# Linear attention with an FP4 feed-forward block on Trainium2: all of gate ahead of all of up in each half, and a tanh that waits for gate alone

## The chip, the cores and the metric

The kernel runs on one core of a Trainium2 chip. The metric is the device time of one execution in microseconds (us); lower is better. Engines are named as the profile names them: PE is the matmul engine and PEld its weight load, DVE the vector engine, ACT the scalar engine, POOL GpSimd and SP the engine that issues the DMAs. DVEq is DVE's instruction queue: the entries that DVE's sequencer carries out itself (register arithmetic, waits, branches) before or between the instructions that it hands to the datapath. All times, counts and rows in this part are those of the kernel before.

## The reference

`x` has 8 sequences of 2048 tokens of 256 features. With `xn = layernorm(x)` the output is `x + attention(xn) + ffn(xn)`. The change lies in the feed-forward part:

```python
def fp4_linear(x, w):                        # quantize both to FP4 in blocks of 16, then multiply
    xq = fp4_quant_dequant(x)
    wq = fp4_quant_dequant(w)
    return jnp.einsum('bsk,nk->bsn', xq, wq)
gate = fp4_linear(x, w_gate)                 # 256 -> 704
y = fp4_linear(x, w_up)                      # 256 -> 704
h = jax.nn.silu(gate) * y
return fp4_linear(h, w_down)                 # 704 -> 256
```

The attention part is a causal linear attention with 16 heads of 16, in buckets of 64 tokens: softmax over q's features, exp of k, running sums of k and of k times v over the earlier buckets.

## The kernel before

The 16384 tokens are cut into 128 tiles of 128. Everything is written out by hand: each engine has one program of its own, in it a function `step(n, d)`, and semaphores with computed thresholds join the programs. A step serves several tiles at once, each at another stage: while tile k is multiplied by the gate and up weights, tile k-1 is quantized for the down projection, k+1 is projected to q, k and v, and k+2 to k+4 are normalised and quantized. Steps come in pairs (d = 0 and 1, for the two parities of the buffers). The first and last pairs are written out, and the 60 pairs between are the body of a loop: `with dve.Fori(2, NP - 2) as n` at L1004 for DVE. In a loop body the threshold of a wait depends on the loop's counter, so a register has to be worked out for it; outside of loops it is a constant.

The feed-forward of one tile goes in two halves of 352 columns. For each half:

- PE (`gate_up`, L1120) multiplies the tile, in two chunks of 128 features, by gate and up. `three_passes` (L1020) makes three matmuls per chunk and per weight, since value and weight are each split in a high and a low part. Gate's sum stands in one PSUM bank (`unit0a` or `unit1a`), up's in another (`unit0b` or `unit1b`). That is twelve matmuls for a half; the last one raises `gu_done` by one.
- ACT (`tanh_gate`, L552) waits for `gu_done` and for `ga_done` of the tile before, reads gate's bank and writes `th`.
- DVE (`gate_h`, L728) waits for tanh and makes `ga` = (th + 1) * gate; DVE (`times_up`, L738) waits for `ga_done` and makes `h` = `ga` * up.

In DVE's step the two halves stand far apart: `gate_h(k, 0)`, then three instructions of other tiles, `times_up(k, 0)`; and at the end of the step `gate_h(k, 1)`, `attention(k, par, 3)` (L723, writes `att`), `times_up(k, 1)` (L744, writes `h`). With d = 1 `times_up(k, 1)` is the last instruction of the loop's body, and what follows it is the loop's turn: register arithmetic and a branch at L1004, and the first entries of the next pass, which lead to `scale_x` (L871 to L876, writes `xq_s`).

In PE's step the second half is cut in two: chunk 0 (six matmuls), `less_xn` (L1049, one matmul that waits for ACT's `split_xnt`), chunk 1 (six matmuls). In ACT's step `tanh_gate(k, 0)` comes behind `exp_q(k + 1)` (L534, `qexp`), which waits for DVE's `shift_q` (L697, `qsh`), and `tanh_gate(k, 1)` behind both `split_xnt(k + 2)` (L513, `xnt`).

Of the semaphores that an instruction waits for it carries one itself; the others are given to entries of their own ahead of it in the queue: to the register operation that works out a threshold, where one stands there, or to an EVENT_SEMAPHORE.

Of the kernel before, what the change touches and what calls it, by code (L numbers as in the profile page):

```python
# [5 lines left out]
def linear_attention_fp4_ffn_block(nc, x, wqkv_t, wout_t, wgate, wup, wdown, out):  # L6
# [18 lines left out]
    P = 128  # L25
# [7 lines left out]
    KC = D // P  # L33
# [7 lines left out]
    FH = F // 2  # L41
# [25 lines left out]
    with ctx:  # L67
        def sb(name, shape, dt=fp32):
            return ctx.enter_context(nc.sbuf_tensor(name, shape, dt))

        def pb(name):
            return ctx.enter_context(nc.psum_tensor(name, [P, 512], fp32))

        def sem(name):
            return ctx.enter_context(nc.semaphore(name))
# [9 lines left out]
        w_gate = sb("w_gate", [P, 2, KC, F], fp16)  # L85
        w_up = sb("w_up", [P, 2, KC, F], fp16)
# [60 lines left out]
        xqt = sb("xqt", [P, 2, 2, D], fp16)  # L147
# [17 lines left out]
        unit = [[pb("unit0a"), pb("unit0b")], [pb("unit1a"), pb("unit1b")]]  # L165
# [51 lines left out]
        gu_done = sem("gu_done")  # L217
# [16 lines left out]
        def after(t, per=1, nth=None):  # L234
            nth = per if nth is None else nth
            if isinstance(t, int):
                return 0 if t < 0 else NT * per if t >= NT else t * per + nth
            return t * per + nth


        def turned(t, par):
            return t * 8 + (16 - 8 * par)

        def begun(t):
            return not isinstance(t, int) or t >= 0


        def is_tile(t):
            return not isinstance(t, int) or 0 <= t < NT
# [14 lines left out]
        def _(sp):  # L264
# [35 lines left out]
            def turn_xq(t, par):  # L300
                if not is_tile(t):
                    return
                sp.wait_ge(xq_step, after(t, 8))
                sp.sem_inc(sp_turn, 1)
                if begun(t - 2):
                    sp.wait_ge(gu_done, after(t - 2, 2))
                sp.sem_inc(sp_turn, 1)
                sp.dma_start_transpose(xqt[:, par, :, :].rearrange("p s (c k) -> p (s c) k", k=P),
                                       xq_s[:, par, :, :].rearrange("p s k -> p (s k)")).then_inc(xqt_done[par], 16)
# [11 lines left out]
            def turn(i):  # L321
                for d in range(2):
                    turn_xq(2 * i + d + 1, 1 - d)
                    turn_h(2 * i + d - 1, 1 - d)
# [8 lines left out]
            last = NT // SEQ_TILES - 1  # L333
# [108 lines left out]
        def _(act):  # L442
# [109 lines left out]
            def tanh_gate(t, half, par):  # L552
                if not is_tile(t):
                    return
                act.wait_ge(gu_done, after(t, 2, half + 1))
                if begun(t - 1):
                    act.wait_ge(ga_done, after(t - 1, 2, half + 1))
                nc.scalar.activation(th[:, half, :], unit[(par + half) % 2][0][:, 0:FH], ACT.Tanh, scale=c_g[:, :])\  # L558
                    .then_inc(tanh_done, 1)
# [16 lines left out]
            def step(n, d):  # L576
                k, par, odd = 2 * n + d, d, 1 - d
                split_att(k - 1, odd, 0)
                exp_k(k + 1, odd)
                split_att(k - 1, odd, 1)  # L580
                exp_q(k + 1, odd)
                tanh_gate(k, 0, par)
                split_xnt(k + 2, par, 0)
                normalise_waits(k + 3)
                mean_waits(n, d + 4)
                split_xnt(k + 2, par, 1)
                tanh_gate(k, 1, par)
                normalise(n, d + 3)
                mean_of(n, d + 4)
                squares_wait(k + 4)  # L590
                copy_qt(k + 1, odd)
                squares_of(n, d + 4)
                snapshot(k + 1)
# [36 lines left out]
        def _(dve):  # L630
# [107 lines left out]
            def times_up(t, half, par):  # L738
                if not is_tile(t):
                    return  # L740
                dve.wait_ge(ga_done, after(t, 2, half + 1))
                if begun(t - 2):
                    dve.wait_ge(hq_step, after(t - 2, 14, 8))
                nc.vector.tensor_tensor(h[:, par, half * FH:(half + 1) * FH], ga[:, half, :],  # L744
                                        unit[(par + half) % 2][1][:, 0:FH], ALU.mult).then_inc(h_done, 1)
# [162 lines left out]
            def step(n, d):  # L908
                k, par, odd = 2 * n + d, d, 1 - d
                scale_x(k + 1, odd)  # L910
                block_max_x(k + 2, par)
                block_max_h(k - 1, odd)
                block_scales(k - 1, odd, k + 2, par)
                max_q(k + 1, odd)
                over_scales_h(k - 1, odd)
                shift_q(k + 1, odd)
                add_up(n, d - 3, 0)
                round_h(k - 1, 0)
                over_scales_x(k + 2, par)
                round_h(k - 1, 1)  # L920
                add_up(n, d - 3, 1)
                round_h(k - 1, 2)
                gate_h(k, 0, par)
                row_factor(k - 1, odd)
                round_x(k + 2, 0)
                times_up(k, 0, par)
                round_x(k + 2, 1)
                attention(k, par, 0)
                scale_h(k - 1, odd, 0)
                scale_h(k - 1, odd, 1)  # L930
                round_x(k + 2, 2)
                attention(k, par, 1)
                attention(k, par, 2)
                gate_h(k, 1, par)
                attention(k, par, 3)
                times_up(k, 1, par)
# [56 lines left out]
            cols = lambda c, i: q_cols[:, c, i * F:(i + 1) * F].rearrange("p (o b i) -> p o b i", i=2, b=FB)  # L993
# [19 lines left out]
        def _(pe):  # L1013
# [6 lines left out]
            def three_passes(outs, stat_hi, stat_lo, hi, lo, first, last):  # L1020

                for o, m in zip(outs, hi):
                    nc.tensor.matmul(o, stat_hi, m, start=first, stop=False)  # L1023
                for o, m in zip(outs, lo):
                    nc.tensor.matmul(o, stat_hi, m, start=False, stop=False)  # L1025
                for o, m in zip(outs, hi):
                    end = nc.tensor.matmul(o, stat_lo, m, start=False, stop=last)  # L1027
                return end
# [88 lines left out]
                nc.tensor.matmul(tr32, minus16[:, :], att_t[:, par, 0, :], start=False, stop=True, skip_group_check=True)\  # L1117
                    .then_inc(att_less, 1)

            def gate_up(t, half, par, chunks=range(KC)):  # L1120
                if not is_tile(t):
                    return
                gate, up = unit[(par + half) % 2]
                pe.wait_ge(xqt_done[par], turned(t, par))
                if half == 0:
                    if begun(t - 1) and 0 in chunks:
                        pe.wait_ge(h_done, after(t - 1, 2))
                elif 0 in chunks:
                    pe.wait_ge(q_shift, after(t + 1))
                    pe.wait_ge(kv_done, after(t + 1, 3))  # L1130
                cols = slice(half * FH, (half + 1) * FH)
                for c in chunks:
                    hi, lo = ((w_gate[:, s, c, cols], w_up[:, s, c, cols]) for s in range(2))
                    last = three_passes((gate[:, 0:FH], up[:, 0:FH]), xqt[:, par, 0, c * P:(c + 1) * P],
                                        xqt[:, par, 1, c * P:(c + 1) * P], hi, lo, c == 0, c == KC - 1)
                if KC - 1 in chunks:
                    last.then_inc(gu_done, 1)

            def project_att(t, par):
# [20 lines left out]
            def step(n, d, ends=False):  # L1160
                k, par, odd = 2 * n + d, d, 1 - d
                project_qkv(k + 1, odd)
                transpose_att(k - 1, odd)
                bucket(k, par, ends)
                less_att(k - 1, odd)
                gate_up(k, 0, par)
                transpose_xn(k + 2, par)
                gate_up(k, 1, par, (0,))
                less_xn(k + 2, par)
                gate_up(k, 1, par, (1,))  # L1170
                transpose_q(k + 1, odd)
                project_att(k - 2, par)
                project_h(k - 2, par)
# [6 lines left out]
            for n in range(2):  # L1180
# [3 lines left out]
                for part in range(2):  # L1184
                    pe.wait_ge((mat_hi, mat_lo)[part][n], 1)
                    for c in range(KC):
# [4 lines left out]
                        for r in range(WR):  # L1191
                            last = nc.tensor.transpose(bank[:, r * WP:(r + 1) * WP],
                                                       q_rows[0:WP, n, part, r * D + c * P:r * D + (c + 1) * P],
                                                       ident16[0:WP, 0:WP])
# [3 lines left out]
            for i, starts in enumerate(([m * P for m in range(0, 4)], [m * P for m in range(4, 8)],  # L1198
# [7 lines left out]
                for m, at in enumerate(starts):  # L1206
                    for c in range(KC):
                        last = nc.tensor.transpose(bank[0:width, m * D + c * P:m * D + (c + 1) * P],
                                                   q_cols[:, c, at:at + width], ident16[:, :])
# [53 lines left out]
```

## Time and profile before

| | us |
|---|---|
| median of 3 runs | 1497.29 (1495.11 to 1497.63) |
| the profiled execution, its own time | 1495.11 |
| span of the profiled execution, first to last instruction | 1493.3 |
| busy in it: DVE / PE / ACT | 1434.4 / 1382.8 / 1011.0 |
| PE's granted clock, mean over the span | 0.988 |

The profile comes from one execution, the fastest of the three runs. Its own time is 1.8 us more than its span. Busy times of instructions that overlap in the pipeline are merged, so the busy time of an engine is the part of the span in which it had at least one instruction under way.

### The profile page before, as it was taken

The page shows a single profiled execution, that of the slowest core. Times are in us where ns is not written, and L with a number is a line of the kernel's source. Part 1 is how long each engine was busy: PE and PEld are TensorE (multiplying, and loading weights), DVE is VectorE, ACT ScalarE, POOL GpSimd, SP SyncE. Part 2 cuts the span into 40 slices and gives each one's busy share as a digit, 9 for nine tenths or more (in the row PEclk, how much of TensorE's full clock was granted, in tenths as well). Part 3 has the DMA queues.
Part 4 walks back from the last instruction along what each step waited for, and adds up shares of the span by engine and source line. Part 5 has one row for each costly group of instructions (what it writes and reads, how often), then busy time and mean ns, then how long its engine had stood idle before and what let it go on. Part 6 is the DMA issues. An engine that isn't in the chain of part 4 may idle for free.

```text
span 1493.3 us, 43457 instructions
## 1 busy us (share of the span) xinstructions
PE 1382.8 (93%) x10702; PEld 948.7 (64%) x10702; DVE 1434.4 (96%) x4914; ACT 1011.0 (68%) x3096; POOL 175.8 (12%) x540
## 2 busy tenths in 40 slices
PE   0259999999999999999999999999999999999997
PEld 0136666666666666666666666666666666666664
DVE  5859999999999999999999999999999999999997
ACT  1687767676767677676767676767767676767662
POOL 1520101010101101010101010110101010101000
PEclk9969999999999999999999999999999999999998
DMA  5002233333332333333333323333333333233324
GB/s 114 4 7 55 63 65 77 69 63 74 70 76 58 81 68 70 64 81 68 63 71 74 72 58 78 68 70 64 81 68 69 65 77 71 61 73 70 71 47 78
DMA packets 293241, 100.01 MB, mean 67 GB/s; under 512 B 258272, under 2 KB 292704, under 8 KB 293216
## 3 DMA queue, kind: packets, MB, share of 16 engines
q1 hardware_dynamic: 293216, 99.73, 31.8%
q8 instruction: 9, 0.15, 0.0%
q14 instruction: 16, 0.13, 0.0%
HBM read 19.99 MB, written 16.78 MB: 25 GB/s over the span
## 4 chain that ended last, share of the span: by engine, by line
DVE 53%; issue 34%; DVEq 7%; ACT 3%; PE 1%; SPq 1%; DMA 0%; POOL 0%; ACTq 0%; POOLq 0%
DVE q_rows L863 5%; DVE osum L900 4%; DVE hw L825 4%; DVE xblk L758 3%; DVE h L744 3%; DVE xw L843 2%; DVE hu L829 2%; DVE hq L835 2%; DVE hv L807 2%; DVE xq_s L876 2%; DVE att L723 1%; DVE xblk L777 1%; DVE qsh L697 1%; DVE hs_lo L883 1%; DVE xblk L769 1%
## 5 line engine op out<-in xcount | busy, mean ns | idle before, releaser
L1154 PE MATMUL outp<-w_down_cat,q_rows 128*128 128x256 f16 x1408 | 246.2, 274 | 0.0
L573 ACT ACTIVATE snap<-ctxp,mask 64x68 f32<-64x68 f32 x1024 | 236.2, 308 | 3.2
L550 ACT ACTIVATE att_t<-trp 128x256 f16<-128x256 f32 x256 | 98.3, 384 | 134.0 <-PE trp L1109 129.6
L534 ACT ACTIVATE qexp<-qsh,c_q 128x256 f32<-128x256 f32 x128 | 65.1, 508 | 147.4 <-DVE qsh L697 147.3
L398 POOL TENSOR_TENSOR var_scaled<-squares,var_mul 128x1 f32<-128x1 f32 x128 | 24.8, 194 | 1188.4 <-ACT scratch L488 1181.7
L1154 PEld LDWEIGHTS outp<-w_down_cat,q_rows 128*128 128x128 f16 x1408 | 138.3, 98 | 16.5
L1156 PE MATMUL outp<-w_down_lo,q_rows 128*128 128x256 f16 x640 | 147.6, 274 | 0.0
L513 ACT ACTIVATE xnt<-trp 128x256 f16<-128x256 f32 x256 | 96.8, 378 | 57.3 <-PE trp L1049 57.3
L751 DVE TENSOR_REDUCE hblk<-h 128x44 f32<-128x704 f32 x128 | 123.6, 966 | 0.1
L807 DVE TENSOR_TENSOR hv<-h,hblk 128x704 f32<-128x704 f32 x128 | 112.7, 881 | 0.0
L558 ACT ACTIVATE th<-unit1a,c_g 128x352 f32<-128x352 f32 x128 | 69.7, 545 | 36.3 <-PE unit1b L1027 36.3
L1087 PE MATMUL nump<-snap,qt 128*64 128x144 f32 x1024 | 91.0, 299 | 3.2 <-ACT snap L573 3.2
L558 ACT ACTIVATE th<-unit0a,c_g 128x352 f32<-128x352 f32 x128 | 69.8, 545 | 29.7 <-PE unit0b L1027 29.7
L1041 PE MATMUL trp<-ident,xn 128*128 128x128 f32 x256 | 49.4, 275 | 37.7 <-ACT xn L504 37.7
L1023 PE MATMUL unit0a<-w_gate,xqt 128*128 128x352 f16 x256 | 80.5, 315 | 3.4 <-DVE qsh L697 1.2
L1023 PE MATMUL unit1a<-w_gate,xqt 128*128 128x352 f16 x256 | 80.5, 314 | 2.9
L504 ACT ACTIVATE xn<-xring,shift,rstd 128x256 f32 (+1 forms) x128 | 75.3, 589 | 11.1 <-POOL shift L408 11.1
L1023 PE MATMUL unit1b<-w_up,xqt 128*128 128x352 f16 x256 | 80.0, 313 | 0.0
L1025 PE MATMUL unit1b<-w_up,xqt 128*128 128x352 f16 x256 | 80.0, 313 | 0.0
L1023 PE MATMUL unit0b<-w_up,xqt 128*128 128x352 f16 x256 | 80.0, 313 | 0.0
L1027 PE MATMUL unit1b<-w_up,xqt 128*128 128x352 f16 x256 | 80.0, 313 | 0.0
L1027 PE MATMUL unit0a<-w_gate,xqt 128*128 128x352 f16 x256 | 80.0, 313 | 0.0
(214 smaller groups left out, 4409.2 us busy)
## 6 DMA issues: line engine op xcount, KB each, us to landing
xring<-x SPq DMA_DIRECT2D x128, 128.0 KB, 2.7
out<-xring SPq DMA_DIRECT2D x128, 128.0 KB, 2.5
xqt<-xq_s SPq DMA_TRANSPOSE x128, 2.4
q_rows<-q_rows SPq DMA_TRANSPOSE x128, 3.5
raw_qkv<-wqkv_t SPq DMA_DIRECT2D x1, 768.0 KB, 7.7
raw_gate<-wgate SPq DMA_DIRECT2D x8, 88.0 KB
raw_up<-wup SPq DMA_DIRECT2D x8, 88.0 KB
raw_down<-wdown SPq DMA_DIRECT2D x1, 704.0 KB, 6.2
```

Source lines behind the costliest of these rows:

```text
L513: nc.scalar.activation(xnt[:, par, part, :], tr32, ACT.Copy).then_inc(xnt_split, 1)
L550: nc.scalar.activation(att_t[:, par, part, :], tr32, ACT.Copy).then_inc(att_split, 1)
L558: nc.scalar.activation(th[:, half, :], unit[(par + half) % 2][0][:, 0:FH], ACT.Tanh, scale=c_g[:, :])\
L573: nc.scalar.activation(kept[:, :, cols], sums[:, :, cols], ACT.Copy, scale=mask[rows, f, h:h + 1])\
L751: nc.vector.tensor_reduce(hblk[:, 0, :], h[:, par, :].rearrange("p (o b i) -> p b o i", b=FB, i=2), AX.XY, ALU.max, apply_absolute_value=T ...
L807: nc.vector.tensor_tensor(rows(hv[:, :]), rows(h[:, par, :]), pairs_of(hblk[:, 2, :]), ALU.mult)\
L1023: nc.tensor.matmul(o, stat_hi, m, start=first, stop=False)
L1025: nc.tensor.matmul(o, stat_hi, m, start=False, stop=False)
L1027: end = nc.tensor.matmul(o, stat_lo, m, start=False, stop=last)
L1087: last = nc.tensor.matmul(nump[rows, g * 2 * SW:(g + 1) * 2 * SW], qt[:, par, g * P + s * BUCKET:g * P + (s + 1) * BUCKET], snap[:, g, s, ...
L1154: nc.tensor.matmul(downp, hqt[:, par, m, :], w_down_cat[:, m, :], start=(m == 0), stop=False)
L1156: nc.tensor.matmul(downp, hqt[:, par, m, :], w_down_lo[:, m, :], start=False, stop=False)
```

## The change

In each half all six gate matmuls now come first and all six up matmuls after them, each group with an increment of `gu_done` at its end: four for each tile instead of two. The parameter `chunks` of `gate_up` becomes `ups`, so the second half is now cut between gate and up instead of between the chunks. Tanh waits for gate's increment. Since tanh no longer stands for up being done, `times_up` gets a wait of its own for up's increment. SP's wait ahead of a transpose into `xqt` names the same moment by its new number.

```diff
 (turn_xq, SP)
-                    sp.wait_ge(gu_done, after(t - 2, 2))
+                    sp.wait_ge(gu_done, after(t - 2, 4))
...
 (tanh_gate, ACT)
-                act.wait_ge(gu_done, after(t, 2, half + 1))
+                act.wait_ge(gu_done, after(t, 4, 2 * half + 1))
...
 (times_up, DVE)
                 dve.wait_ge(ga_done, after(t, 2, half + 1))
+                dve.wait_ge(gu_done, after(t, 4, 2 * half + 2))
                 if begun(t - 2):
                     dve.wait_ge(hq_step, after(t - 2, 14, 8))
...
 (PE)
-            def gate_up(t, half, par, chunks=range(KC)):
+            def gate_up(t, half, par, ups=(0, 1)):
...
-                gate, up = unit[(par + half) % 2]
+                pair = unit[(par + half) % 2]
...
-                for c in chunks:
-                    hi, lo = ((w_gate[:, s, c, cols], w_up[:, s, c, cols]) for s in range(2))
-                    last = three_passes((gate[:, 0:FH], up[:, 0:FH]), xqt[:, par, 0, c * P:(c + 1) * P],
-                                        xqt[:, par, 1, c * P:(c + 1) * P], hi, lo, c == 0, c == KC - 1)
-                if KC - 1 in chunks:
+                for up in ups:
+                    for c in range(KC):
+                        hi, lo = ((w_gate, w_up)[up][:, s, c, cols] for s in range(2))
+                        last = three_passes((pair[up][:, 0:FH],), xqt[:, par, 0, c * P:(c + 1) * P],
+                                            xqt[:, par, 1, c * P:(c + 1) * P], (hi,), (lo,), c == 0, c == KC - 1)
                     last.then_inc(gu_done, 1)
```

The first place is PE's loop, the second half of a tile with d = 1 (`unit0a` gate, `unit0b` up; L1049 is `less_xn`). Before:

```order
L1130 ISA [waits q_shift,xqt_done1]
L1023 MATMUL unit0a<-w_gate,xqt 128x352 [waits kv_done]
L1023 MATMUL unit0b<-w_up,xqt 128x352
L1025 MATMUL unit0a<-w_gate,xqt 128x352
L1025 MATMUL unit0b<-w_up,xqt 128x352
L1027 MATMUL unit0a<-w_gate,xqt 128x352
L1027 MATMUL unit0b<-w_up,xqt 128x352
L1048 ISA
L1049 MATMUL trp<-xnt,minus 128x256 [waits xnt_split]
L1023 MATMUL unit0a<-w_gate,xqt 128x352 [waits xqt_done1]
```

And of the change, whose lines are one higher from here on:

```order
L1131 ISA [waits q_shift,xqt_done1]
L1024 MATMUL unit0a<-w_gate,xqt 128x352 [waits kv_done]
L1026 MATMUL unit0a<-w_gate,xqt 128x352
L1028 MATMUL unit0a<-w_gate,xqt 128x352
L1024 MATMUL unit0a<-w_gate,xqt 128x352
L1026 MATMUL unit0a<-w_gate,xqt 128x352
L1028 MATMUL unit0a<-w_gate,xqt 128x352
L1049 ISA
L1050 MATMUL trp<-xnt,minus 128x256 [waits xnt_split]
L1024 MATMUL unit0b<-w_up,xqt 128x352 [waits xqt_done1]
```

All of gate stands ahead of `less_xn` and all of up behind it; number, size and waits of the matmuls are the same.

The second place is DVE's loop, the end of its body with the loop's turn (`ga` and `h` are those of the second half). Before:

```order
L731 REGISTER_ALU
L734 SCALAR_TENSOR_TENSOR ga<-th,unit0a 128x352 [waits h_done,tanh_done]
L720 REGISTER_ALU
L723 TENSOR_TENSOR att<-nump,drec 128x256 [waits att_tr,att_step]
L744 TENSOR_TENSOR h<-ga,unit0b 128x352 [waits hq_step,ga_done]
L1004 REGISTER_ALU
L1004 COMPARE_AND_BRANCH
```

And of the change:

```order
L731 REGISTER_ALU
L734 SCALAR_TENSOR_TENSOR ga<-th,unit0a 128x352 [waits h_done,tanh_done]
L720 REGISTER_ALU
L723 TENSOR_TENSOR att<-nump,drec 128x256 [waits att_tr,att_step]
L742 REGISTER_ALU [waits ga_done]
L745 TENSOR_TENSOR h<-ga,unit0b 128x352 [waits hq_step,gu_done]
L1005 REGISTER_ALU
L1005 COMPARE_AND_BRANCH
```

Of the two semaphores that `h` had, the wait for `ga_done` has gone to a new register operation ahead of it, which works out the threshold for `gu_done`; `h` now has `hq_step` and `gu_done`. The second half of a tile with d = 0 changes in the same way.

The third place is DVE's loop, `times_up` of the first half with d = 0. Before:

```order
L842 REGISTER_ALU
L843 TENSOR_SCALAR xw<-xv 128x256 [waits xq_step]
L743 REGISTER_ALU [waits ga_done]
L744 TENSOR_TENSOR h<-ga,unit0b 128x352 [waits hq_step]
L846 ISA
```

And of the change:

```order
L843 REGISTER_ALU
L844 TENSOR_SCALAR xw<-xv 128x256 [waits xq_step]
L742 ISA [waits ga_done]
L744 REGISTER_ALU [waits gu_done]
L745 TENSOR_TENSOR h<-ga,unit0b 128x352 [waits hq_step]
L847 ISA
```

Here one entry is added between the wait for `ga_done` and `h`.

## Rows read from the trace of the kernel before

**Rows 1.** The page, parts 1 and 4: busy time; the chain that ended last.
```profile
PE 1382.8 (93%) x10702; PEld 948.7 (64%) x10702; DVE 1434.4 (96%) x4914; ACT 1011.0 (68%) x3096; POOL 175.8 (12%) x540
...
DVE 53%; issue 34%; DVEq 7%; ACT 3%; PE 1%; SPq 1%; DMA 0%; POOL 0%; ACTq 0%; POOLq 0%
```

**Rows 2.** Waits of DVE, whole span: who for whom, total us, times, longest.
```profile
DVE qmax L688 <- PE unit1b L1027: 15.2, 1, 15.2
...
DVE ga L734 <- ACT th L558: 2.8, 3, 2.4
```

**Rows 3.** Waits of ACT between 200 and 1400 us.
```profile
ACT th L558 <- PE unit1b L1027: 29.7, 56, 0.5
ACT th L558 <- PE unit0b L1027: 24.1, 56, 0.4
```

**Rows 4.** Timeline of ACT, one step: start, us, instruction, idle before and releaser.
```profile
706.34 0.51 ACT L534 ACTIVATE qexp<-qsh,c_q 128x256 f32<-128x256 f32 x1 [1.21 <-DVE qsh L697]
706.75 0.54 ACT L558 ACTIVATE th<-unit0a,c_g 128x352 f32<-128x352 f32 x1
...
708.91 0.55 ACT L558 ACTIVATE th<-unit1a,c_g 128x352 f32<-128x352 f32 x1 [0.53 <-PE unit1b L1027]
```

**Rows 5.** Timeline of PE in the same step.
```profile
704.22 0.31 PE L1023 MATMUL unit0a<-w_gate,xqt 128*128 128x352 f16 x1
704.37 0.31 PE L1023 MATMUL unit0b<-w_up,xqt 128*128 128x352 f16 x1
...
705.86 0.31 PE L1027 MATMUL unit0b<-w_up,xqt 128*128 128x352 f16 x1
...
709.51 0.27 PE L1154 MATMUL outp<-w_down_cat,q_rows 128*128 128x256 f16 x1
709.62 0.27 PE L1156 MATMUL outp<-w_down_lo,q_rows 128*128 128x256 f16 x1
```

**Rows 6.** Timeline of DVE, second half with d = 0, no turn behind it.
```profile
711.28 0.52 DVE L734 SCALAR_TENSOR_TENSOR ga<-th,unit1a 128x352 f32<-128x352 f32 x1
...
712.05 0.51 DVE L744 TENSOR_TENSOR h<-ga,unit1b 128x352 f32<-128x352 f32 x1
712.48 0.28 DVE L874 TENSOR_TENSOR xq_s<-xq,xs_hi 128x256 f16<-128x256 f16 x1
```

**Rows 7.** Timeline of DVE, second half with d = 1, the loop's turn behind it.
```profile
700.43 0.52 DVE L734 SCALAR_TENSOR_TENSOR ga<-th,unit0a 128x352 f32<-128x352 f32 x1
...
701.20 0.51 DVE L744 TENSOR_TENSOR h<-ga,unit0b 128x352 f32<-128x352 f32 x1
701.74 0.29 DVE L874 TENSOR_TENSOR xq_s<-xq,xs_hi 128x256 f16<-128x256 f16 x1
```

**Rows 8.** The chain that ended last, at that turn: start, us, what.
```profile
700.55 0.02 DVEq L722
...
700.66 0.02 DVEq L743
...
701.07 0.06 DVEq L1004
...
701.53 0.05 DVEq L871
...
701.63 0.06 DVEq L873
```

**Rows 9.** Line 1004: count, least/median/most ns of one, first and last start.
```profile
L1004 DVEq COMPARE_BRANCH  x60: 50/56/67, 161.7 to 1434.4; - x60
```

**Rows 10.** The chain between 711.78 and 712.7 us, no turn.
```profile
711.93 0.04 DVEq L871
...
712.02 0.05 DVEq L873
```

**Rows 11.** Timelines of ACT and DVE at the first tile.
```profile
103.83 0.51 ACT L534 ACTIVATE qexp<-qsh,c_q 128x256 f32<-128x256 f32 x1
105.67 0.56 ACT L558 ACTIVATE th<-unit0a,c_g 128x352 f32<-128x352 f32 x1 [1.33 <-PE unit0b L1027]
...
106.26 0.52 DVE L734 SCALAR_TENSOR_TENSOR ga<-th,unit0a 128x352 f32<-128x352 f32 x1 [2.37 <-ACT th L558]
...
108.37 0.52 DVE L734 SCALAR_TENSOR_TENSOR ga<-th,unit1a 128x352 f32<-128x352 f32 x1 [0.20 <-ACT th L558]
```

More of the change, by code:

```diff
@@ L1118, in less_att @@
                     .then_inc(att_less, 1)
-            def gate_up(t, half, par, chunks=range(KC)):
+            def gate_up(t, half, par, ups=(0, 1)):
                 if not is_tile(t):
                     return
-                gate, up = unit[(par + half) % 2]
+                pair = unit[(par + half) % 2]
                 pe.wait_ge(xqt_done[par], turned(t, par))
                 if half == 0:
-                    if begun(t - 1) and 0 in chunks:
+                    if begun(t - 1) and 0 in ups:
                         pe.wait_ge(h_done, after(t - 1, 2))
-                elif 0 in chunks:
+                elif 0 in ups:
                     pe.wait_ge(q_shift, after(t + 1))
```

## The prediction

> **What bounds the kernel now.** I read the page first, then who waited for whom, then the timeline of one step, and last DVE's own queue.
>
> The page names the engine: DVE is busy for 1434.4 of 1493.3 us and the chain that ended last runs over DVE for more than half of its length, with 34% of "issue" and 7% of DVEq in it [rows 1]. The list of DVE's waits shows that nobody makes it wait in the steady part: 15.2 us for the first projection and 2.8 us in three places for tanh are the kind of entry it has [rows 2], and between 200 and 1400 us the list is empty. What the reader is to see there: tanh, which the change serves earlier, is not what DVE waits for.
>
> ACT does wait for the last up matmul: 29.7 + 24.1 = 53.8 us in 112 places, 0.48 us each [rows 3]. The timeline says which half: the second tanh begins 0.53 us after ACT came free. The first has no wait for PE: it stands behind `qexp`, which begins at 706.34 because DVE's `qsh` came so late, while the last up matmul of that half ended at 705.86 + 0.31 = 706.17 [rows 4, 5]. And the second tanh ends at 708.91 + 0.55 = 709.46, 1.82 us before its reader `ga` begins at 711.28 [rows 4, 6].
>
> So DVE goes by its own pace, and that has two parts. Mostly an instruction begins about 0.08 us before the recorded end of the one before: h 712.05 + 0.51 = 712.56, next at 712.48 [rows 6]. There the datapath is the limit. At the loop's turn it is not: h 701.20 + 0.51 = 701.71, next at 701.74 [rows 7]. There is a hole of 0.03 where the pattern has an overlap of 0.08: 0.11 us are lost, with the branch and the two waits of L871 and L873 in the queue all through it [rows 8]. That happens 60 times [rows 9]. Here DVE's sequencer is the limit, and whatever delays the sequencer delays DVE one for one.
>
> **What starts the turn.** `ga` ends at 700.43 + 0.52 = 700.95. The wait of L743 (for `hq_step`) is over at 700.66, `h` itself then waits for `ga_done`, and the branch starts only at 701.07, 0.12 after `ga`'s end; in between is only the register operation of L1004. From the branch to `xq_s` it is 701.74 - 701.07 = 0.67 [rows 7, 8]. So the turn is a chain that begins at the end of `ga`: 0.12 + 0.67 = 0.79.
>
> **The change, part by part.**
>
> *Matmuls.* As many, of the same size, with the same weight loads. New is that six in a row add to one bank. Before they alternate at 704.37 - 704.22 = 0.15 us for 352 columns; the down projection adds to one bank all the time, at 709.62 - 709.51 = 0.11 for 256 [rows 5]. Both are 0.43 ns a column, so one bank in a row costs nothing. Bound from the other side: 0.01 us of reading error in each of 24 matmuls is 0.24 us a tile, on an engine that DVE's chain never waits for. I take 0.
>
> *Tanh earlier.* In the first half nothing moves, as `qexp` is in front. In the second it may begin when `split_xnt` lets ACT go, 0.53 us earlier; that fills 128 times ACT idle time, and the work behind it moves up. DVE takes `th` 1.82 us after it is there, so the steady part gains 0. If that cover were gone it would be worth 0.53 x 128 = 68 us.
>
> *Start-up.* Here DVE does wait for tanh: 2.37 us and then 0.20 [rows 11]. In the first tile ACT is free of `qexp` at 103.83 + 0.51 = 104.34; gate's six matmuls end about 6 x 0.15 = 0.9 us before up's last, so tanh comes 0.9 us earlier and DVE's first `ga` too. Of that the second half lets through 0.5 (its tanh gains about 0.53, as in the steady step), and the three places hold 2.8 - 2.37 - 0.20 = 0.2 more. I take a gain of 1.0 us, once; the bounds are 0.5 and 1.5.
>
> *The added wait on DVE.* `times_up` gets a third semaphore. What matters is what stands behind `ga_done`, since that is where the sequencer is held. At the turn it was the push of `h` alone. Now, with `ga_done` moved to the new register operation, there follow that operation, an entry that waits for `hq_step` (satisfied long before, as at 700.66) and then `h` with `gu_done` (satisfied too: up ended microseconds ago). Two entries more between `ga`'s end and the branch. The price of one: two register operations in a row start 712.02 - 711.93 = 0.09 apart [rows 10], and L871 to L873 0.10; two waits with the push of `att` between them 700.66 - 700.55 = 0.11 [rows 8], of which the push takes the 0.02 above 0.09. So 0.09 + 0.09 = 0.18 us: the branch starts 0.30 after `ga`'s end and `xq_s` 0.97 after it. The hole is open already, so all of it lengthens the pass: 0.18 x 60 = 10.8 us.
>
> Does `h` itself become late? Its register operation starts some 0.04 after `ga`'s end, the wait 0.09 later, and from the end of the last entry to the start of its instruction it is 701.74 - 701.69 = 0.05 at the turn [rows 7, 8]. That puts `h` at 0.04 + 0.09 + 0.02 + 0.05 = 0.20 after `ga`'s end. It begins at 701.20 - 700.95 = 0.25 now, and 712.05 - 711.80 = 0.25 with d = 0 [rows 6, 7]: 0.05 to spare, hidden under `att`. Without a turn behind it the queue then has until 712.48, 0.68 after `ga`'s end, and needs the three entries of `scale_x`: also hidden. In the first halves `h` stands two instructions further back. Cost 0, but with little to spare in the second halves.
>
> *SP's and ACT's waits* name the same or an earlier moment; an entry more on ACT, which has a third of its time idle, costs 0.
>
> **The sum**: -1.0 + 10.8 = +9.8 us. Against the profiled execution's own 1495.11 us that is 1504.9 (span 1503.1); the median of the runs shown lies 2.2 us higher, so 1497.3 + 9.8 = 1507.1.
>
> **A rule weighed.** The rows show the sequencer held by the wait that `h` carries: the wait ahead of it is over at 700.66, yet the branch comes at 701.07, 0.12 after `ga`'s end [rows 8]. The Trainium skill ("Perfetto Trace Analysis", section "DVE / Act Engine Instruction") says that an instruction goes to a wait queue and the sequencer is ready for the next at once. By that rule the turn before would have started at about 700.66 + 0.1, no hole would be seen, and only the change would tie it to `ga`: xq_s at 0.97 after 700.95 = 701.92 instead of 701.63, 0.29 x 60 = 17.4, less 1.0: 1513.7 us. The trace has the hole already, so I go by the rows.
>
> **The rivals.**
>
> *Hidden after all* (no change): the extra entries run while the sequencer would have waited for something else, such as the fetch behind the branch, and the turn keeps its 0.79. The gap between branch and L871, 0.46 us with one entry in it, speaks for some slack there; that the branch follows `ga` so closely speaks against it. Then only the start-up's gain is left: 1496.3. A middle form has one entry hidden and one not: 0.09 x 60 - 1.0 = +4.4, 1501.7.
>
> *Dearer*: the entries cost 0.05 more than I take, so that `h` is late in each of 128 steps: 0.05 x 128 = 6.4 on top, 1513.5, or the skill's wait queue with its 1513.7.
>
> *Faster*: ACT's 0.53 us a tile reach DVE. That needs DVE to wait for ACT in the steady part; it decides from 1.82 us less lead of `th`. If a tenth of the tiles did, it would be 0.53 x 13 = 6.8 us: with the start-up's 1.0 and no cost at the turn, 1489.5. Nothing in [rows 2] speaks for it.
>
> *Matmuls into one bank slower*: PE would have to lose more than its stalls of a step. The down projection's pace excludes it nearly.
>
> **How the numbers follow.** The forecast (1504 to 1510) has 0.66, the middle form 0.09, dearer 0.08, no change 0.13, faster 0.04. A change of under 0.2% (3 us) can't be told from none here. The forecast, the dearer case and nearly all of the middle form are slower: 0.82; same 0.14; faster 0.04. The range of 8 in 10 takes in the middle form and most of the dearer: 1500.5 to 1513.
>
> **What would show it.** In the profile after: at the turn the branch starts about 0.30 after `ga`'s end and `xq_s` about 0.97, with a hole of about 0.21 between `h` and `xq_s`; the same place without a turn keeps its overlap of 0.08 and `h` its 0.25; ACT's idle time before the second tanh is gone and turns up before `att_t` or `qexp`; the first `ga` begins 0.9 us earlier. It is wrong if the branch still starts 0.12 after `ga`'s end, or if holes appear at the other second half.

## The result, and the profile after

The changed kernel takes 1505.22 us (median of 5 runs, 1504.33 to 1506.02) against 1497.5 for the kernel before (5 runs, 1495.11 to 1497.75) in the same comparison: ratio 1.0052, 95% interval 1.0038 to 1.0066. It is slower by 7.7 us. Its profiled execution took 1506.02 us, the slowest of the five, with a span of 1504.3.

The page of the changed kernel, parts 1 and 4:

```profile
PE 1383.2 (92%) x10702; PEld 950.0 (63%) x10702; DVE 1434.3 (95%) x4914; ACT 995.3 (66%) x3096; POOL 185.4 (12%) x540
...
DVE 51%; issue 36%; DVEq 8%; ACT 2%; PE 1%; SPq 1%; DMA 0%; POOL 0%; ACTq 0%; POOLq 0%
```

DVE has the same work (1434.3 us against 1434.4 in [rows 1]) in a span that is 11.0 us longer, and the share of "issue" and DVEq in the chain has grown from 41 to 44%. So the time is between DVE's instructions. The list of DVE's waits says where:

```profile
DVE xq_s L875 <- issue: 11.7, 59, 0.2
...
DVE ga L734 <- ACT th L558: 3.0, 2, 2.4
```

The first of these rows is new: 59 holes of 0.20 us in front of `xq_s`, which is what follows the loop's turn. In [rows 2] the list has no such row, since the holes of before are only 0.03 long. The other row is the start-up, no shorter than before.

The turn itself, as the timeline of DVE in the changed kernel (start, us, instruction, idle before and releaser) and as the chain (start, us, what) have it:

```profile
705.49 0.52 DVE L734 SCALAR_TENSOR_TENSOR ga<-th,unit0a 128x352 f32<-128x352 f32 x1
...
706.26 0.51 DVE L745 TENSOR_TENSOR h<-ga,unit0b 128x352 f32<-128x352 f32 x1
706.97 0.29 DVE L875 TENSOR_TENSOR xq_s<-xq,xs_hi 128x256 f16<-128x256 f16 x1 [0.20 <-issue]
```

```profile
706.13 0.02 DVEq L744
...
706.22 0.04 DVEq L1005
...
706.62 0.09 DVEq L1005
```

`ga` ends at 705.49 + 0.52 = 706.01. Before, the wait for `hq_step` (L743) was over long before `ga`'s end [rows 8]; now (L744) it comes at 706.13, 0.12 behind it. The register operation of the turn starts at 706.22; the branch, which the chain leaves out here, starts 0.07 after it, 0.29 after `ga`'s end in each of the 60 turns. `xq_s` starts 0.96 after `ga`'s end, against 0.79 [rows 7]; from the third turn to the 59th this agrees to 0.01 (the first two are longer by 0.04 and 0.01, and no jump follows the last). `h` still starts 706.26 - 706.01 = 0.25 after `ga`'s end. And the second half without a turn behind it is as it was in [rows 6]:

```profile
716.51 0.52 DVE L734 SCALAR_TENSOR_TENSOR ga<-th,unit1a 128x352 f32<-128x352 f32 x1
...
717.28 0.51 DVE L745 TENSOR_TENSOR h<-ga,unit1b 128x352 f32<-128x352 f32 x1
717.71 0.28 DVE L875 TENSOR_TENSOR xq_s<-xq,xs_hi 128x256 f16<-128x256 f16 x1
```

The sum over the loop is (0.20 - 0.03) x 60 = 10.2 us. The branches themselves give nearly the same. In the changed kernel their row is

```profile
L1005 DVEq COMPARE_BRANCH  x60: 50/56/67, 162.8 to 1445.4; - x60
```

From the first to the last it is 1282.6 us, against 1272.7 in [rows 9]. So 9.9 of the 11.0 us between the two spans lie in the loop, and 1.1 ahead of its first branch; behind the last branch both kernels take 58.9.

ACT did get what the change is about. In its timeline the second tanh (713.50) follows `xnt` without a gap, and the list of its waits between 200 and 1400 us has no row for `th` any more [rows 3]; the time has gone to other waits (`att_t` had 110.2 us before, `qexp` 131.7):

```profile
713.22 0.38 ACT L513 ACTIVATE xnt<-trp 128x256 f16<-128x256 f32 x1 [0.43 <-PE trp L1050]
713.50 0.55 ACT L558 ACTIVATE th<-unit1a,c_g 128x352 f32<-128x352 f32 x1
```

```profile
ACT att_t L550 <- PE trp L1110: 175.3, 110, 1.6
ACT qexp L534 <- DVE qsh L697: 141.6, 111, 1.4
```

The start-up, one row of PE before, then rows of PE, ACT and DVE in the changed kernel's timeline:

```profile
103.67 0.32 PE L1023 MATMUL unit0a<-w_gate,xqt 128*128 128x352 f16 x1
```

```profile
103.53 1.23 PE L1088 MATMUL nump<-snap,qt 128*64 128x144 f32 x8
104.54 1.12 PE L1098 MATMUL ctxp<-vaug,kexp 128*64 128x136 f32 x8
...
105.60 0.32 PE L1024 MATMUL unit0a<-w_gate,xqt 128*128 128x352 f16 x1
...
106.70 0.55 ACT L558 ACTIVATE th<-unit0a,c_g 128x352 f32<-128x352 f32 x1 [1.40 <-PE unit0a L1028]
...
107.29 0.52 DVE L734 SCALAR_TENSOR_TENSOR ga<-th,unit0a 128x352 f32<-128x352 f32 x1 [2.44 <-ACT th L558]
...
109.18 0.55 ACT L558 ACTIVATE th<-unit1a,c_g 128x352 f32<-128x352 f32 x1
...
109.77 0.52 DVE L734 SCALAR_TENSOR_TENSOR ga<-th,unit1a 128x352 f32<-128x352 f32 x1 [0.56 <-ACT th L558]
```

The first tanh comes 1.10 us after the first gate matmul. Before it was 2.00: the first gate matmul of the first tile started at 103.67 there, and tanh at 105.67 [rows 11]. So 0.9 us were gained at that place. The second tanh stands behind `xnt`, which waits for PE's `less_xn`, so DVE now waits 0.56 us for it instead of 0.20 [rows 11]. The second `ga` starts 109.77 - 105.60 = 4.17 us after the first gate matmul, where it was 108.37 - 103.67 = 4.70. The third `ga`, which had a short wait for tanh before and has none now, starts 11.22 after it instead of 12.09. These distances are the same in the traces of the runs below: the third `ga` comes after 12.08 or 12.09 us in all six that keep tanh waiting for up, and after 11.21 or 11.22 in the five that have the change's tanh (the run with the other three waits moved aside, with 11.55). So the start-up gains 0.9 us from the first gate matmul on.

It doesn't show in the profiled execution because PE came to the first gate matmul later, at 105.60 instead of 103.67. PE was at the lower clock (1.2 GHz, granted 0.5) for 30.7 us ahead of it in this execution and for 27.3 in the profiled one of before, and the two groups of eight matmuls took 1.23 and 1.12 us instead of 0.71 and 0.63. `ga` therefore came at 107.29 instead of 106.26. The traces don't put the length of that stretch down to the change: among the traces that keep tanh waiting for up (the kernel before and six runs) it is 27.3 us in three and 30.7 in four, with the first gate matmul anywhere from 103.66 to 105.37, and a run with the change's tanh has 27.3 as well (two more behind the hold).

### The profile page after: what moved, and what is told of

The parts are those of the page before. It is cut to its first block, busy times and chain, and to the rows that moved or that the text cites. A ratio compares the mean times of both kernels' runs of the same rounds, so it can differ in the third digit from the quotient of the medians.

```text
span 1504.3 us, 43581 instructions
## 1 busy us (share of the span) xinstructions
PE 1383.2 (92%) x10702; PEld 950.0 (63%) x10702; DVE 1434.3 (95%) x4914; ACT 995.3 (66%) x3096; POOL 185.4 (12%) x540
## 4 chain that ended last, share of the span: by engine, by line
DVE 51%; issue 36%; DVEq 8%; ACT 2%; PE 1%; SPq 1%; DMA 0%; POOL 0%; ACTq 0%; POOLq 0%
DVE q_rows L864 5%; DVE osum L901 4%; DVE hw L826 4%; DVE xblk L759 3%; DVE xw L844 2%; DVE hu L830 2%; DVE hv L808 2%; DVE xq_s L877 2%; DVE h L745 2%; DVE xblk L778 1%; DVE qsh L697 1%; DVE hs_lo L884 1%; DVE att L723 1%; DVE ga L734 1%; DVE xblk L770 1%
## 5 line engine op out<-in xcount | busy, mean ns | idle before, releaser
L398 POOL TENSOR_TENSOR var_scaled<-squares,var_mul 128x1 f32<-128x1 f32 x128 | 37.7, 294 | 1188.9 <-ACT scratch L488 1181.6
L1024 PE MATMUL unit1a<-w_gate,xqt 128*128 128x352 f16 x256 | 80.5, 314 | 13.2 <-DVE qsh L697 13.2
L504 ACT ACTIVATE xn<-xring,shift,rstd 128x256 f32 (+1 forms) x128 | 76.5, 597 | 11.6 <-POOL shift L408 11.6
L1026 PE MATMUL unit0b<-w_up,xqt 128*128 128x352 f16 x256 | 80.0, 313 | 0.0
L1026 PE MATMUL unit1a<-w_gate,xqt 128*128 128x352 f16 x256 | 80.0, 313 | 0.0
L1028 PE MATMUL unit1a<-w_gate,xqt 128*128 128x352 f16 x256 | 80.0, 313 | 0.0
L1026 PE MATMUL unit1b<-w_up,xqt 128*128 128x352 f16 x256 | 80.0, 313 | 0.0
L1024 PE MATMUL unit0b<-w_up,xqt 128*128 128x352 f16 x256 | 80.0, 313 | 0.0
L1028 PE MATMUL unit1b<-w_up,xqt 128*128 128x352 f16 x256 | 80.0, 313 | 0.0
```

The lines of the kernel that those rows point to most:

```text
L504: nc.scalar.activation(xn[:, d % 2, :], xring[:, (n + d // 2) % XCH, d % 2, :], ACT.Identity, bias=shift[:, d % 2, :], scale=rstd[:, d % 2 ...
```

## Experiments

Three theories were on record. T1: the cost is the entries in DVE's queue between the end of `ga` and the branch of the turn. T2: each of the 256 added waits costs a little wherever it stands. T3: the cost is in the order of the matmuls. All runs of one group were compared with the kernel before on the same chip; its median was 1496.28 (21 runs) for the first four, 1495.62 (10 runs) for the next four and 1495.66 (15 runs) for the last four.

**The order alone.** Gate ahead of up, one increment for each half, at up's end:

```diff
 (against the change)
+                if 1 in ups:
                     last.then_inc(gu_done, 1)
 (and the waits of SP, ACT and DVE as before)
```

> All of gate ahead of all of up, but one increment of gu_done for each half, at up's end; tanh waits for that one and DVE has no wait of its own for it. Theory T1 (the cost is two more entries in DVE's queue between the end of ga and the branch of the loop's turn): the turn is as before, branch 0.12 us after ga's end, hole 0.03, time that of before, 1497.5 within 1.5. T2 (each of the 256 added waits costs some 0.04 us wherever it stands): also 1497.5. T3 (the cost is in the matmuls' order: one bank in a row, or what PE and ACT then do): 1505.

Measured: 1495.96 us, ratio 0.9997 (0.9988 to 1.0006). In the trace the branch starts 0.12 after `ga`'s end and there is no row for `xq_s` in DVE's waits. T3 falls: six matmuls in a row into one bank cost nothing that can be measured here.

**The waits alone.** The order of before, an increment at the end of each chunk:

```diff
 (against the kernel before; SP's wait as in the change)
-                act.wait_ge(gu_done, after(t, 2, half + 1))
+                act.wait_ge(gu_done, after(t, 4, 2 * half + 2))
...
                 dve.wait_ge(ga_done, after(t, 2, half + 1))
+                dve.wait_ge(gu_done, after(t, 4, 2 * half + 2))
...
-                if KC - 1 in chunks:
                     last.then_inc(gu_done, 1)
```

> The matmuls in the order of before, with an increment of gu_done at the end of each chunk, so four for each tile; tanh waits for the second of its half as before; DVE's times_up has the change's third wait. T1 and T2: 1505 to 1507, branch 0.29 after ga's end, hole 0.20. T3: 1497.5.

Measured: 1506.04 us, ratio 1.0064 (1.0050 to 1.0077), the whole cost. DVE's waits have the row of the changed kernel:

```profile
DVE xq_s L875 <- issue: 11.6, 59, 0.2
```

**One of the four waits moved.** The change, with the wait for up ahead of `dmx` instead of ahead of `h`, in the second half of d = 1 only:

```diff
-                dve.wait_ge(gu_done, after(t, 4, 2 * half + 2))
+                if (half, par) != (1, 1):
+                    dve.wait_ge(gu_done, after(t, 4, 2 * half + 2))
...
+            def up_wait(t, half):
+                if is_tile(t):
+                    dve.wait_ge(gu_done, after(t, 4, 2 * half + 2))
...
                 round_x(k + 2, 2)
+                if d == 1:
+                    up_wait(k, 1)
                 attention(k, par, 1)
```

> The change, with one of its four added waits for up in the pair of steps moved: that of the second half with d = 1, the one ahead of the loop's turn, now stands three instructions earlier (ahead of dmx), so that h waits for hq_step and ga_done as before. T1: the whole cost goes, branch 0.12 after ga's end, hole 0.03, 1495.5 to 1497.5. T2: a quarter of the cost goes, 1503. T3: 1505.

Measured: 1496.57 us, ratio 1.0002 (0.9992 to 1.0011): the whole cost is gone with one wait in four. The timeline and the chain at the turn of this run:

```profile
701.17 0.52 DVE L734 SCALAR_TENSOR_TENSOR ga<-th,unit0a 128x352 f32<-128x352 f32 x1
...
702.48 0.29 DVE L880 TENSOR_TENSOR xq_s<-xq,xs_hi 128x256 f16<-128x256 f16 x1
```

```profile
701.39 0.02 DVEq L745
...
701.81 0.06 DVEq L1012
```

The wait of L745 (`hq_step`) is over ahead of `ga`'s end at 701.69 again, and the branch comes at 701.81, 0.12 after it. The moved wait and its register operation are still carried out, four instructions earlier (`dmx`, `drec`, `ga` and `att` now stand between it and `h`), ahead of the hold.

**The other three moved.**

```diff
 (up_wait as in the run before)
-                dve.wait_ge(gu_done, after(t, 4, 2 * half + 2))
+                if (half, par) == (1, 1):
+                    dve.wait_ge(gu_done, after(t, 4, 2 * half + 2))
...
+                up_wait(k, 0)
                 round_h(k - 1, 2)
                 gate_h(k, 0, par)
...
                 round_x(k + 2, 2)
+                if d == 0:
+                    up_wait(k, 1)
                 attention(k, par, 1)
```

> The reverse of the run before: the three other waits are moved away from between ga_done and h, the one ahead of the turn is left as in the change. T1: nothing goes, branch 0.29 after ga's end, 1505. T2: three quarters of the cost go, 1499.5. T3: 1505.

Measured: 1505.55 us, ratio 1.0059 (1.0045 to 1.0073). Nothing is won. In the timeline of this run `ga` ends at 704.91 + 0.52 = 705.43 and `xq_s` comes 0.96 later, with the hole of the change:

```profile
704.91 0.52 DVE L734 SCALAR_TENSOR_TENSOR ga<-th,unit0a 128x352 f32<-128x352 f32 x1
...
706.39 0.29 DVE L880 TENSOR_TENSOR xq_s<-xq,xs_hi 128x256 f16<-128x256 f16 x1 [0.20 <-issue]
```

T2 falls: the two runs together put all of the cost at the one place.

**More ahead of the hold.** The kernel before with a satisfied wait more at the turn:

```diff
                 dve.wait_ge(ga_done, after(t, 2, half + 1))
+                if (half, par) == (1, 1):
+                    dve.wait_ge(tanh_done, after(t, 2, 2))
```

> The kernel before with one more wait at the loop's turn, for tanh_done, which is satisfied already; it gets an entry of its own, but h still carries the wait for ga_done, so the entry stands ahead of the place at which the sequencer is held. T1: it is carried out while the sequencer would be waiting for ga anyway, branch 0.12 us after ga's end, time that of before, 1496. If an entry costs 0.09 a turn wherever it stands: 5.2 us, 1501.

Measured: 1495.45 us, ratio 0.9997 (0.9988 to 1.0006). The edit gave less than I meant: no entry of its own, but a second semaphore in the entry that waits for `hq_step`, which now lasts 0.05 instead of 0.02 (the chain of this run):

```profile
701.51 0.05 DVEq L745
...
701.93 0.06 DVEq L1006
```

It stands ahead of `ga`'s end (701.81) and the branch keeps its 0.12. That a whole entry ahead of the hold is free is shown by the run with the one wait moved, not by this one.

**More behind the hold.** The change with two satisfied waits more at the turn:

```diff
                 dve.wait_ge(gu_done, after(t, 4, 2 * half + 2))
+                if (half, par) == (1, 1):
+                    dve.wait_ge(num_done, after(t))
+                    dve.wait_ge(xn_done, after(t))
```

> The change with two more waits at the turn, for num_done and xn_done, both long satisfied, behind the wait for ga_done. T1: two entries more behind the hold, branch 0.29 + 0.17 = 0.46 us after ga's end, hole 0.37, another 10.2 us: 1515.5.

Measured: 1510.43 us, ratio 1.0098 (1.0083 to 1.0114), 14.8 us above the kernel before where the two runs above that have the change's turn are 9.3 and 9.8 above it. The chain and the timeline of this run:

```profile
707.10 0.02 DVEq L745
707.16 0.05 DVEq L747
...
707.36 0.06 DVEq L1008
```

```profile
706.45 0.52 DVE L734 SCALAR_TENSOR_TENSOR ga<-th,unit0a 128x352 f32<-128x352 f32 x1
...
707.26 0.52 DVE L748 TENSOR_TENSOR h<-ga,unit0b 128x352 f32<-128x352 f32 x1
708.02 0.29 DVE L878 TENSOR_TENSOR xq_s<-xq,xs_hi 128x256 f16<-128x256 f16 x1 [0.25 <-issue]
```

My 1515.5 was too high since the two waits became one entry more, not two: L747 holds two semaphores. The branch starts 0.39 after `ga`'s end at 706.97, so this one entry costs 0.10, 6 us over 60 turns; measured are some 5 (1510.43 against 1505.2 to 1506.0 for the three kernels with the change's turn). The price for each entry behind the hold thus stands twice: 0.17 for two, 0.10 for one. `h` is late here too, by 0.04 (0.29 after `ga`'s end), and that does no harm by itself, as the turn's chain lasts longer.

**The turn elsewhere.** The same instructions in the same order, but the loop's body begins two instructions later in it (first on the kernel before, then on the change):

```diff
             def step(n, d):
...
-                scale_x(k + 1, odd)
                 block_max_x(k + 2, par)
...
                 times_up(k, 1, par)
+                scale_x(k + 2, par)
```

> The kernel before with scale_x of the next step moved into the end of DVE's step: the same instructions in the same order, but the loop's turn lies behind both xq_s instead of behind h. T1: the turn's entries run while DVE still has about 0.8 us of work pushed, the hole goes wholly, 0.11 x 60 = 6.6 us faster: 1490. If the turn costs what it costs wherever it lies (rival): 1496.3.

> The same on the change. T1: the entries start 0.17 us later than in the run on before, which uses up the margin of 0.14 there; a hole of at most 0.04 us is left: 1490 to 1493. Rival: 1505.

Measured: 1488.25 us, ratio 0.9951 (0.9937 to 0.9964), and on the change 1488.19, ratio 0.9950 (0.9936 to 0.9963). Both beat both kernels, and the change costs nothing any more. Timeline and chain of the run on the change:

```profile
719.12 0.52 DVE L734 SCALAR_TENSOR_TENSOR ga<-th,unit0a 128x352 f32<-128x352 f32 x1
...
719.89 0.51 DVE L745 TENSOR_TENSOR h<-ga,unit0b 128x352 f32<-128x352 f32 x1
720.32 0.28 DVE L875 TENSOR_TENSOR xq_s<-xq,xs_hi 128x256 f16<-128x256 f16 x1
720.52 0.28 DVE L877 TENSOR_TENSOR xq_s<-xq,xs_lo 128x256 f16<-128x256 f16 x1
720.72 0.41 DVE L759 TENSOR_REDUCE xblk<-xn 128x16 f32<-128x256 f32 x1
```

```profile
719.76 0.02 DVEq L744
...
720.22 0.06 DVEq L1005
```

The branch now starts 0.58 after `ga`'s end (719.64), as the entries of `scale_x` come first, but DVE has `h` and both `xq_s` under way or pushed, and `xblk` overlaps its predecessor by 0.08 like everything else. The hole that I thought possible on the change isn't there. The gain of 7.4 us on the kernel before is the 0.11 x 60 = 6.6 that was expected, or a little more: in the traces the loop takes 1265.9 us from its first to its last branch (162.6 to 1428.5), 6.8 less than in [rows 9].

**The turn later still**, behind the longest instruction, on the change:

```diff
-                scale_x(k + 1, odd)
-                block_max_x(k + 2, par)
-                block_max_h(k - 1, odd)
...
                 times_up(k, 1, par)
+                scale_x(k + 2, par)
+                block_max_x(k + 3, odd)
+                block_max_h(k, par)
```

> The change with scale_x, block_max_x and block_max_h of the next step moved into the end of DVE's step, so the turn lies behind the longest instruction, hblk with 0.97 us. T1: no hole is left in either parity, 1490; the waits that the change added cost nothing there.

Measured: 1491.43 us, ratio 0.9971 (0.9959 to 0.9983). There is no hole at the turn, but it is 3 us slower than the run before it. Its first `ga` comes at 108.36 us, against 106.64 there. So 1.7 of the 4.2 us between the spans of the two traces (1490.7 and 1486.5) lie ahead of the loop. The moved instructions come before the preparation of the weights there, which may be the reason; neither that nor the rest was followed up.

**Fewer turns.** Loop bodies of four and of six steps on DVE, on the change (e5) and on the kernel before (e11, e12):

```diff
-            with dve.Fori(2, NP - 2) as n:
-                for d in range(2):
-                    step(n, d)
+            with dve.Fori(1, NP // 2 - 1) as m:
+                for j in range(2):
+                    for d in range(2):
+                        step(2 * m + j, d)
```

With six steps it is `dve.Fori(0, (NP - 4) // 3) as m`, three values of `j` and `step(3 * m + (2 + j), d)`.

> The change, with DVE's loop body made of four steps instead of two: 30 turns instead of 60, the added waits all in place. T1: 30 of 60 times the turn's hole of 0.28 us (0.20 and the missing overlap of 0.08) goes, 8.4 us: 1497. If only what the change added came 60 times whatever the turns (T2), only before's own 0.11 a turn would go: 3.3 us, 1502. More registers for four steps could cost either a little.

> The kernel before with DVE's loop body of four steps, 30 turns. The run with such a body on the change had 3.8 us between branch and next entry at each turn. If the length of the body does it (L): the same 3.8 here, about 1617. If the change's waits or registers do it (R): 0.32 as before and 30 holes fewer, 1493.

> The kernel before with a body of six steps, 20 turns. L with a fixed price of each turn: 20 x 3.8, about 1575. L with a price that grows with the body's length: 5.7 a turn, about 1610. R: 1492.

Measured: 1626.93 us (ratio 1.0878), 1628.13 (1.0877) and 1563.97 (1.0455). T1's 1497 for the first was far off, and the reason isn't in the change, as the kernel before shows the same. The timeline and the chain at a turn of the kernel before with four steps:

```profile
709.52 0.51 DVE L744 TENSOR_TENSOR h<-ga,unit0b 128x352 f32<-128x352 f32 x1
713.71 0.29 DVE L874 TENSOR_TENSOR xq_s<-xq,xs_hi 128x256 f16<-128x256 f16 x1 [3.69 <-issue]
```

```profile
709.39 0.06 DVEq L1004
...
713.50 0.05 DVEq L871
```

From branch to L871 it is 4.11 us, against 0.46 in [rows 8]. DVE's waits of the runs with four and with six steps:

```profile
DVE xq_s L874 <- issue: 106.2, 29, 3.9
DVE qmax L688 <- PE unit0b L1028: 15.9, 29, 0.7
...
DVE ga L734 <- ACT th L558: 11.6, 32, 2.4
```

```profile
DVE xq_s L874 <- issue: 70.9, 19, 3.8
```

3.66 and 3.73 us a turn: the price is the same for four steps and for six, so it is paid for each jump back over a long body and doesn't grow with it. With six steps (3.73 - 0.03) x 20 - 0.11 x 40 = 69.6 us against 68.3 measured. With four the holes give (3.66 - 0.03) x 30 - 0.11 x 30 = 105.6 of the 132.5. Most of the other 27 are the two rows below it, 15.9 us and what 11.6 exceeds the 2.8 of [rows 2] by: DVE then waits for PE and ACT. PE's mean granted clock is 0.928 there instead of 0.988. After the turn shown, PE is busy for only 1.14 of the 3.30 us from 713.70 to 717.00, and from 717 to 724 its granted clock is 0.51, so matmuls behind such a pause run at 1.2 GHz. With four steps such a stretch of 6.8 us follows each of the 29 jumps; with six it is 3.4 us behind 18 of 19, and DVE hardly waits for PE.

What comes with the long pause is code. Part 3 of a page counts DMA packets of the kind "instruction" (packets, MB, share of the DMA engines). One row each from the pages of the kernel before, of it with four steps and of it with six:

```profile
q14 instruction: 16, 0.13, 0.0%
q14 instruction: 163, 1.33, 0.2%
q14 instruction: 133, 1.09, 0.2%
```

That is (163 - 16) / 29 = 5.1 more for each jump back with four steps and (133 - 16) / 19 = 6.2 with six; the changed kernel has 16 as well. In the trace one of these packets starts in every pause between branch and next entry with four steps, in most about 2.1 us after the branch, and in every one with six, while there is none at any of the 59 jumps of the kernel before. Only DVE's program differs between these kernels. So the pause is most likely DVE waiting for its own instructions, fetched again at each jump back; the packets don't name their engine, so this is argued and not shown.

## Why the prediction was right, point by point

**What bounds the kernel.** Right. DVE's work is unchanged to 0.1 us, and the 53.8 us that ACT waited for up's end went into other waits of ACT.

**What starts the turn.** Right: with one wait moved ahead the branch follows `ga` by 0.12 again, with one entry more it follows by 0.39.

**The price of the added wait.** Two entries, predicted at 0.18, measured 0.17: branch 0.29 instead of 0.30, `xq_s` 0.96 instead of 0.97, hole 0.20 instead of 0.21. The sum of the term was 10.8 us and is 10.2. The medians give 7.7 for the change and, with the same turn, 9.8 (waits alone, without the start-up's gain) and 9.3 (other three moved). The kernel before itself had medians from 1495.6 to 1497.5 in the four comparisons, so the 2 us between these are not to be told from noise.

**`h` isn't late.** Right, 0.25 after `ga`'s end in both parities, and with one entry more it is 0.29: the 0.05 to spare were as small as worked out.

**Matmuls at 0.** Right (order alone, 0.9997).

**Start-up, -1.0 us.** Right in mechanism and nearly in size: 0.53 us at the second `ga` and 0.87 at the third, counted from the first gate matmul, inside the bounds of 0.5 and 1.5. The prediction's working is weaker than its number: what it names behind the 0.9 of the first tanh is 0.5 for the second half and 0.2 for the other places, which makes 0.7 and not the 1.0 that it takes. And the gain can't be seen in the times: in the profiled execution the first gate matmul came 1.93 us later, and that moment scatters by 1.7 us among the traces that keep tanh waiting for up. The turn-later pair, change against before, differs by 0.06 us, and the change with one wait moved is 0.3 us slower than the kernel before, with an interval from -1.2 to +1.6 us, so 1 us more or less is below what these medians can tell.

**The rule weighed.** The trace of the kernel before speaks against the wait queue that the Trainium skill describes ("Perfetto Trace Analysis", section "DVE / Act Engine Instruction"): there too the branch follows `ga`'s end by 0.12, in all 60 turns, though `h` carries the wait. The time agrees: 1505.2 and not the 1513.7 worked out by that rule.

**The rivals.** Hidden after all, wholly or one of the two: no, the entries show one for one. Dearer: no, `h` keeps its 0.25. Faster: no `th` row in DVE's steady part. The time, 1505.2 against 1507.1 forecast, lies inside the range. That it came out 1.9 below is within the scatter of the medians.

## What to carry to other kernels

On an engine that never waits for others, look at the places where the sequencer is held, by a wait for the engine's own latest result, with a loop's turn behind: each entry there, a register operation or a wait already satisfied, was paid in full here at each pass, while the same entry four instructions earlier, ahead of the hold, was free. Put waits that are surely satisfied ahead of such a hold, and put the turn of the loop behind long instructions that don't wait for the one just before; that gave 0.5% here for moving one call. Saving turns by a longer body has to be measured: here it cost 3.7 us for each turn.

## What the runs showed of the hardware that was not expected

- A DVE loop whose body has four or six steps (about 336 and 504 records of DVE between two branches) lost 3.66 and 3.73 us at each turn, from branch to next entry 3.9 us, where a body of two steps (169 records) has 0.32. DMA packets of instructions come with it, one in each pause and about five or six more for each jump, where the body of two steps has none at its jumps; that DVE waits for them is argued, not shown. The pause is the same for 336 records as for 504, and the limit between 172 (the longest body without it) and 336 wasn't looked for. PE's, ACT's and POOL's loops in the same traces go on 0.16 to 0.27 us after their branches.
- One wait entry can hold two semaphores and then lasts 0.05 us instead of 0.02, so a second wait there is cheaper than an entry of its own at 0.09 to 0.10.
- At the turn, DVE's register operation and branch start only once the wait that `h` carries itself is over: they come 0.05 and 0.12 us after `ga`'s end in all 60 turns of the kernel before, though the entries ahead of them are done 0.3 us earlier.
